# A Flamingo block on one core: row maxima turned in one instruction and sent in four transfers, softmax denominators kept in 128 columns, the first layer-norm deviations on VectorE

## The reference, cut to what matters

```python
# x, ctx: (4, 1024, 512); 16 heads of 32
q = _layernorm(x).reshape(B, T, 16, 32); k = v = ctx.reshape(B, T, 16, 32)
q = q * cos + rotate_half(q) * sin
k = k * cos + rotate_half(k) * sin
scores = jnp.einsum('bqhd,bkhd->bhqk', q, k) * scale + alibi_bias
attn = jax.nn.softmax(scores, axis=-1)
x = x + jnp.tanh(g_xattn[0]) * jnp.einsum('bhqk,bkhd->bqhd', attn, v)
# then a quantized feed-forward part: w_gate, w_up (1536 x 512) in 4 bits by blocks of 32,
# activations in 16 bits with one scale over the whole tensor, sigmoid in 16 bits, w_down
x = x + jnp.tanh(g_ffn[0]) * ffn(_layernorm(x))
```

## Time and profile before

| what | value |
| --- | --- |
| device time, median of 3 runs | 1749.58 us (1749.09 to 1751.61) |
| the profiled execution | 1751.76 us |
| its span, first to last instruction | 1749.9 us |
| busy share of the span: PE, DVE, ACT, POOL | 92%, 83%, 70%, 48% |
| attention, up to the first step of the feed-forward part | about 918 us |

### The profile page before, as it was taken

How to read it: one execution, slowest core, us unless ns; L and a number is a source line. 1 busy time by engine, 2 the same in 40 slices (tenths; PEclk the granted TensorE clock), 3 DMA queues, 4 the chain that set the end, 5 groups by cost and what they waited for, 6 DMA issues and landing times. The chain is left out here.

```text
span 1749.9 us, 37267 instructions
## 1 busy us (share of the span) xinstructions
PE 1602.6 (92%) x14821; PEld 637.6 (36%) x14821; DVE 1449.6 (83%) x2082; ACT 1221.1 (70%) x1941; POOL 838.9 (48%) x504
## 2 busy tenths in 40 slices
PE   3899999999999999999979999999999950899999
PEld 0233333333333333333325444444444420344444
DVE  7899999999999888888857998868989989755451
ACT  3688888888889888988753332329997987754450
POOL 5699899999999999998740010100000000000000
PEclk9999999999999999999999999999999975899999
DMA  6678889888799787877577898649998999986661
GB/s 156 154 149 174 169 173 182 158 170 173 152 176 182 149 175 160 171 156 140 115 175 189 266 261 271 219 153 324 347 348 275 335 354 387 287 277 216 217 217 60
DMA packets 377182, 367.94 MB, mean 210 GB/s; under 512 B 217872, under 2 KB 288912, under 8 KB 369072
## 3 DMA queue, kind: packets, MB, share of 16 engines
q1 hardware_dynamic: 368080, 300.55, 61.8%
q0 software_dynamic: 8928, 65.02, 19.0%
HBM read 154.08 MB, written 95.42 MB: 143 GB/s over the span
## 5 line engine op out<-in xcount | busy, mean ns | idle before, releaser
L1463 DVE TENSOR_REDUCE cm<-quad 128x1 f16<-128x1024 f32 x512 | 600.2, 1214 | 64.8 <-PE quad L1005 63.9
L1244 ACT ACTIVATE P<-quad 128x512 f32<-128x512 f32 x1024 | 556.8, 598 | 114.0 <-PE quad L1018 102.2
L2072 POOL TENSOR_TENSOR Ps<-P,P 128x2048 f32<-128x2048 f32 x93 | 440.6, 4738 | 45.2 <-ACT P L1244 45.2
L1018 PE MATMUL quad<-QA,KA 101*32 101x512 f16 x4096 | 366.1, 385 | 6.8 <-ACT P L1244 5.3
L1005 PE MATMUL quad<-KA,QA 100*32 100x512 f16 x4096 | 334.3, 391 | 35.6 <-DMA QA<-S 18.1
L1069 PE MATMUL quad<-P,cg 128*32 128x512 f32 x2048 | 265.5, 594 | 0.0
L1097 PE MATMUL quad<-x_hl,Wg 128*128 128x512 f16 (+1 forms) x1200 | 249.1, 370 | 1.3 <-DVE x_hl L1759 1.0
L1097 PE MATMUL quad<-x_hl,Wu 128*128 128x512 f16 x1152 | 248.8, 379 | 0.0
L1158 PE MATMUL quad<-Wd,oh 128*128 128x512 f16 x768 | 228.6, 379 | 0.0
L1018 PEld LDWEIGHTS quad<-QA,KA 101*32 101x32 f16 x4096 | 105.1, 94 | 299.3 <-ACT P L1244 231.1
L1325 ACT ACTIVATE ev<-quad 128x1024 f32<-128x1024 f32 x95 | 96.2, 1013 | 109.3 <-PE quad L1097 103.3
(11 more groups left out here) (169 smaller groups left out, 1938.3 us busy)
## 6 DMA issues: line engine op xcount, KB each, us to landing
Ps<-P POOLq DMA_DIRECT2D x62, 1024.0 KB, 8.1
gate_scratch<-ev SPq DMA_DIRECT2D x48, 512.0 KB, 3.8
gt<-gate_scratch SPq DMA_DIRECT2D x48, 512.0 KB, 5.6
up_scratch<-ev SPq DMA_DIRECT2D x48, 512.0 KB, 4.3
ud<-up_scratch SPq DMA_DIRECT2D x96, 256.0 KB, 3.6
x_words<-up_scratch SPq DMA_DIRECT2D x45, 512.0 KB, 11.4
gated_scratch<-gq SPq DMA_DIRECT2D x48, 256.0 KB, 4.1
gd<-gated_scratch SPq DMA_DIRECT2D x96, 128.0 KB, 4.3
```

What stands on the lines that cost most here:

```text
L1018: mm = e.matmul(K.score[h % 2][j:j + 32, :], K.KA[p % 2][0:101, kt, h, j:j + 32], K.QA[p % 2][0:101, 4 * qc:4 * qc + 4, h, :], start=True, ...
L1244: e.activation(K.Pb[pb][:, h, :], K.score[h % 2], ACT.Exp, scale=SCALE / (QPOW * KPOW)).then_inc(K.a_exp, 1)
L1463: e.tensor_reduce(cm[:, col:col + 1], K.quad[UNIT["max", hm, u] % 2][:, :], AX.X, ALU.max).then_inc(K.v_max, 1)
L2072: e.tensor_tensor(K.Ps[n][:, :, :], K.Pb[(st.g - 1) % NP][:, :, :], K.Pb[st.g % NP][:, :, :], ALU.add).then_inc(K.g_sum, 1)
```

## The change

It has three parts.

1. **Maxima.** `crow` is 128x32; one VectorE transpose over 128 partitions turns each 32x32 block in place of four transposes over 32 partitions, so the rows of queries 32i to 32i+31 lie in partitions 32i and on. Four DMAs carry them, each 16 pieces of 32 values (64 bytes) where one DMA had 16 pieces of 256 bytes. The semaphore `d_crow` counts 64 for a half-task.
2. **Denominators.** In place of ones a matrix `pick` stands (128x4x32, with ones in column `qt` of block `qt`). Each call of `denominators` has four matmuls of 128 queries for each head, where it had one of 512; all add into the same 128 columns, and row `qt` of a head's 32 partitions holds queries 128 `qt` and on. `den` and `denT` have 128 columns, one transpose in place of four turns `denT`, and the reciprocal reads its 16 values at other places.
3. **First deviations.** For the first four row tiles GpSimd does two steps (add, power), and VectorE does five (`first_deviations`), ahead of its step on the bias. For all later tiles nothing changes. GpSimd's other counts on `g_r1` are lower by 8, and `v_first` replaces `v_rope0`.

```diff
@@ -281,7 +281,7 @@
 
 def r1_no(b):
 
-    return 2 * R1 * (b + 1)
+    return 2 * R1 * (b + 1) - BY_VECTOR
 
 
 def w_no(m, k):
@@ -303,6 +303,7 @@
 
 
 R1, R2 = 10, 9
+FIRST, BY_VECTOR = 5, 8
 
 
 def r2_no(b):
...
@@ -350,7 +351,7 @@
 
         self.quad = quad = [ctx.enter_context(nc.psum_tensor(f"quad{i}", [128, 1024], F32)) for i in range(4)]
         self.score = [quad[2][:, 0:512], quad[2][:, 512:1024]]
-        self.num, self.den = quad[3][:, 0:512], quad[3][:, 512:1024]
+        self.num, self.den = quad[3][:, 0:512], quad[3][:, 512:640]
 
         A = Arena(nc)
         self.ident = A("ident", [128, 128], F32)
@@ -382,7 +383,7 @@
 
-        self.ones = A("ones", [128, HD], F32)
+        self.pick = A("pick", [128, 4, HD], F32)
         self.seventh = A("seventh", [128, 1], F32)
@@ -395,12 +396,12 @@
         self.biasT = A("biasT", [128, 8, 4, 16], F16)
         self.numT = A("numT", [128, 512], F32)
-        self.denT = A("denT", [128, 512], F32)
+        self.denT = A("denT", [128, 128], F32)
         self.cm = [A(f"cm{i}", [128, 32], F16) for i in range(2)]
-        self.crow = [A(f"crow{i}", [32, 128], F16) for i in range(2)]
+        self.crow = [A(f"crow{i}", [128, 32], F16) for i in range(2)]
...
@@ -717,9 +718,10 @@
 
     def write_rows(hf):
         p, qc, k = hf // 2, hf % 2, hf % 2
-        e.wait_ge(K.v_row, 4 * hf + 4)
-        row = K.QA[p % 2][100:101, 4 * qc:4 * qc + 4, :, :].rearrange("o i h q -> o (i h) q")
-        e.dma_start(row, K.crow[k][0:16, :]).then_inc(K.d_crow[k], 16)
+        e.wait_ge(K.v_row, hf + 1)
+        for i in range(4):
+            row = K.QA[p % 2][100:101, 4 * qc:4 * qc + 4, :, 32 * i:32 * i + 32].rearrange("o i h q -> o (i h) q")
+            e.dma_start(row, K.crow[k][32 * i:32 * i + 16, :]).then_inc(K.d_crow[k], 16)
 
     def load_weight(m, k):
         z, use, old = K.w_buffer(m, k)
@@ -1013,7 +1015,7 @@
         if n > 2:
             e.wait_ge(K.a_exp, n - 2)
         if kt == 0 and h == 0:
-            e.wait_ge(K.d_crow[hf % 2], 16 * (hf // 2) + 16)
+            e.wait_ge(K.d_crow[hf % 2], 64 * (hf // 2) + 64)
         for j in range(0, 128, 32):
             mm = e.matmul(K.score[h % 2][j:j + 32, :], K.KA[p % 2][0:101, kt, h, j:j + 32],
                           K.QA[p % 2][0:101, 4 * qc:4 * qc + 4, h, :], start=True, stop=True)
@@ -1036,10 +1038,15 @@
                 e.wait_ge(K.g_sum, sum_no(hf, n))
             else:
                 e.wait_ge(K.d_acc[n // 2], 16 * hf + 16)
-        for h in range(4):
-            if (hf, n, h) == (NHALF - 1, 3, 2):
+        Ps, last = K.Ps[n % 2 if hf == NHALF - 1 else n], n == (3 if hf == NHALF - 1 else 2)
+        halves = ((0, 1), (2, 3)) if (hf, n) == (NHALF - 1, 3) else ((0, 1, 2, 3),)
+        for heads in halves:
+            if heads == (2, 3):
                 e.wait_ge(K.v_sum, 5)
-            mm = e.matmul(K.den[32 * h:32 * h + 32, :], K.ones[:, :], K.Ps[n % 2 if hf == NHALF - 1 else n][:, h, :], start=n == 0, stop=n == (3 if hf == NHALF - 1 else 2))
+            for qt in range(4):
+                for h in heads:
+                    mm = e.matmul(K.den[32 * h:32 * h + 32, :], K.pick[:, qt, :], Ps[:, h, 128 * qt:128 * qt + 128],
+                                  start=n == qt == 0, stop=last and qt == 3)
         mm.then_inc(K.pe_den, 1)
 
     before = None
@@ -1071,13 +1078,14 @@
             mm.then_inc(K.pe_pv, 1)
         if st.out is not None:
             hf = st.out
-            for half, src, sem, done in ((0, K.denT, K.a_den, K.pe_tden), (1, K.numT, K.a_num, K.pe_tnum)):
-                ps = K.bank(("out", hf), half)
-                e.wait_ge(*K.bank_release(("out", hf), half))
-                e.wait_ge(sem, hf + 1)
-                for i in range(4):
-                    mm = e.transpose(ps[:, 128 * i:128 * i + 128], src[:, 128 * i:128 * i + 128], ident)
-                mm.then_inc(done, 1)
+            e.wait_ge(*K.bank_release(("out", hf), 0))
+            e.wait_ge(K.a_den, hf + 1)
+            e.transpose(K.bank(("out", hf), 0)[:, 0:128], K.denT[:, :], ident).then_inc(K.pe_tden, 1)
+            e.wait_ge(*K.bank_release(("out", hf), 1))
+            e.wait_ge(K.a_num, hf + 1)
+            for i in range(4):
+                mm = e.transpose(K.bank(("out", hf), 1)[:, 128 * i:128 * i + 128], K.numT[:, 128 * i:128 * i + 128], ident)
+            mm.then_inc(K.pe_tnum, 1)
         if st.s != 1 and st.dens is not None:
             denominators(*st.dens)
         before = st
@@ -1183,9 +1191,9 @@
             n = 8 * b + i
             if i == 0:
                 e.wait_ge(K.d_xg[p % 4], 16 * (p // 4) + 16)
-                e.wait_ge(K.g_r1, R1 if p == 0 else r1_no(b))
+                e.wait_ge(*((K.v_first, FIRST) if p == 0 else (K.g_r1, r1_no(b))))
...
@@ -1459,15 +1467,14 @@
             if hm < 2:
                 e.wait_ge(K.v_cm, hm + 1)
             else:
-                e.wait_ge(K.v_row, 4 * hm - 4)
+                e.wait_ge(K.v_row, hm - 1)
         e.tensor_reduce(cm[:, col:col + 1], K.quad[UNIT["max", hm, u] % 2][:, :], AX.X, ALU.max).then_inc(K.v_max, 1)
 
     def turn_rows(hm):
         e.wait_ge(K.v_max, max_no(hm, 15))
         if hm >= 2:
-            e.wait_ge(K.d_crow[hm % 2], 16 * (hm // 2))
-        for i in range(4):
-            e.transpose(K.crow[hm % 2][:, 32 * i:32 * i + 32], K.cm[hm % 2][32 * i:32 * i + 32, :]).then_inc(K.v_row, 1)
+            e.wait_ge(K.d_crow[hm % 2], 64 * (hm // 2))
+        e.transpose(K.crow[hm % 2][:, :], K.cm[hm % 2][:, :]).then_inc(K.v_row, 1)
 
     def low_part(p, w, half):
         rows = slice(4 * half, 4 * half + 4)
@@ -1506,25 +1513,40 @@
...
+    def first_deviations():
+        mean, rs, nm = K.mv1[:, 0:4, 0], K.rs1[:, 0:4], K.nm1[:, 0:4]
+        shifted, guess, square, factor = [t[:, 0:4] for t in K.nwt]
+        e.wait_ge(K.g_r1, 2)
+        e.tensor_tensor(square, guess, guess, ALU.mult).then_inc(K.v_first, 1)
+        e.wait_ge(K.v_first, 1)
+        e.tensor_tensor(factor, square, shifted, ALU.mult).then_inc(K.v_first, 1)
+        e.wait_ge(K.v_first, 2)
+        e.tensor_scalar(square, factor, -0.5, 1.5, ALU.mult, ALU.add).then_inc(K.v_first, 1)
+        e.wait_ge(K.v_first, 3)
+        e.scalar_tensor_tensor(rs, guess, QPOW / KPOW, square, ALU.mult, ALU.mult).then_inc(K.v_first, 1)
+        e.wait_ge(K.v_first, 4)
+        e.scalar_tensor_tensor(nm, mean, -1.0, rs, ALU.mult, ALU.mult).then_inc(K.v_first, 1)
+
+    first_deviations()
     e.wait_ge(K.pe_bias, 1)
     e.wait_ge(K.a_bias, 1)
     bias = K.score[0][:, 0:256].rearrange("t (i n h) -> t i n h", n=2, h=16)
     e.tensor_tensor(K.biasT[:, :, 2:4, :], bias, K.biasT[:, :, 0:2, :], ALU.subtract).then_inc(K.v_bias, 1)
     e.wait_ge(K.v_cs, 2)
     e.wait_ge(K.d_cg[1], 16)
-    first_rotation(K.cg[1], K.t1[1], slice(0, 8), 0)
+    first_rotation(K.cg[1], K.t1[1], slice(0, 8), FIRST)
     e.wait_ge(K.a_xn, 4)
-    first_rotation(K.xn, K.t1[0], slice(0, 4), 4)
+    first_rotation(K.xn, K.t1[0], slice(0, 4), FIRST + 4)
     low_part(0, 1, 1)
     low_part(0, 0, 0)
     for n in range(4, 8):
@@ -1626,12 +1648,12 @@
             hf = st.out
             p, qc = hf // 2, hf % 2
             y = K.x2s[:, 4 * qc:4 * qc + 4, :]
-            den = K.bank(("out", hf), 0).rearrange("p (i c) -> p i c", c=128)
+            den = K.bank(("out", hf), 0)[:, 0:128].rearrange("p (h c) -> p c h", c=32)
             num = K.bank(("out", hf), 1).rearrange("p (i h d) -> p i h d", i=4, d=HD)
             e.wait_ge(K.pe_tden, hf + 1)
             if hf > 0:
                 e.wait_ge(K.v_x2, hf)
-            e.reciprocal(K.rdn[:, :, :], den[:, :, 0::32]).then_inc(K.v_rec, 1)
+            e.reciprocal(K.rdn[:, :, :], den[:, 0:4, :]).then_inc(K.v_rec, 1)
             e.wait_ge(K.pe_tnum, hf + 1)
             e.wait_ge(K.v_rec, hf + 1)
             if p > 0 and qc == 0:
...
@@ -1940,7 +1962,9 @@
     e.memset(K.minus[:, :], -1.0).then_inc(K.g_half, 1)
     e.memset(K.seventh[:, :], 1.0 / 7.0).then_inc(K.g_half, 1)
     e.memset(K.twice[:, :], QPOW / KPOW).then_inc(K.g_half, 1)
-    e.memset(K.ones[:, :], 1.0).then_inc(K.g_ones, 1)
+    e.memset(K.pick[:, :, :], 0.0).then_inc(K.g_ones, 1)
+    e.wait_ge(K.g_ones, 1)
+    e.memset(K.pick[:, :, :].rearrange("p i c -> p (i c)")[:, 0:4 * HD:HD + 1], 1.0).then_inc(K.g_ones, 1)
 
     def step_of(out, a, b, op, sem, count):
@@ -1961,11 +1985,15 @@
         step_of(rs, nw[1], nw[3], ALU.mult, sem, base + 7)
 
 
+    def first_guesses():
+        e.wait_ge(K.g_half, 6)
+        e.wait_ge(K.v_mv1, 4)
+        step_of(K.nwt[0][:, 0:4], K.mv1[:, 0:4, 1], K.eps[:, 0:4], ALU.add, K.g_r1, 1)
+        step_of(K.nwt[1][:, 0:4], K.nwt[0][:, 0:4], K.half[:, 0:4], ALU.pow, K.g_r1, 2)
+
     def deviation_1(first, last, base):
         c = slice(first, last)
         w = [t[:, 0:last - first] for t in K.nwt]
-        if base == 0:
-            e.wait_ge(K.g_half, 6)
         if first == 20:
 
             e.wait_ge(K.g_r2, R2)
@@ -2034,14 +2062,15 @@
...
```

(33 more changed lines are left out.)

## The result

The change made the kernel slower. The kernel after takes **1837.92 us** (median of 4 runs, 1833.47 to 1846.93), the kernel before 1749.95 us beside it (4 runs, 1749.09 to 1751.61): a ratio of 1.0508, with a 95% interval of 1.0474 to 1.0542. That is 88 us more where 12 us less was forecast, and far outside the range of 1728 to 1748. The profiled execution took 1837.91 us, its span is 1836.1 us.

A forecast was written before the change was run, and what follows sets the result against it. No engine alone bounds the first stage, GpSimd the one between 600 and 800 us. 20 half-tasks at 0.55 us (-11.0), start -1.1, end -0.6, rows +0.7 make -12.0 from 1749.58: 1737.6 us, range 1728 to 1748.

The forecast's parts named there:

- Maxima, transfers: Four row DMAs in place of one bring the last landing 1.0 us later: 0.7 us added in all, bounds 0 and 32.
- The margin: Time between a row's landing and its need by the scores: 3.5 us to spare, 2.5 kept after the delay.
- The 32 us bound: Upper bound on the cost of the four row transfers: 32 x 1.0 us of delay.
- Maxima, VectorE: One transpose of about 0.2 us for four taking 0.90: 0.7 us less a half-task, 0.5 on the path.
- Denominators, TensorE: Small matmuls stay near streaming, 0.11 us a group of four; one transpose for four: 0.3 us less a half-task, 0.2 on path.
- Rival A: TensorE held up by handing over small matmuls in `denominators`, 0.22 us a group: +37 us, 1787 us; chance 0.11.
- ScalarE's copy, start and end: Copy of `den` 0.3 us shorter; first maxima 1.1 us earlier (bounds 0 and 1.8); copy and transposes at the end 0.6 less.
- GpSimd's stage: Between 600 and 800 us GpSimd's own work sets the pace: no gain, reciprocals unchanged at 26.9 us apart.
- Rival C: GpSimd's sums come late in all half-tasks, half of the 0.7 us gain stays: -7.7, 1742 us; chance 0.16.
- Rival B: Gain eaten up by weight loads at 0.14 us a group or rows landing late: 1746 to 1750 us; chance 0.11.

The follow-up runs named there:

- the kernel with the row last: Kernel before, with three idle small transfers issued ahead of the one transfer of the maxima's row: 1869.92 us, ratio 1.0673.
- the kernel with the row first: Kernel before, with three idle small transfers issued right behind the one transfer of the maxima's row: 1750.08 us, ratio 0.9997.
- the adding DMA behind the rotation: Kernel after, with GpSimd's adding DMA issued behind its rotation in the step and not ahead of it: 1768.02 us, ratio 1.0095.

## Why the prediction was wrong

- **Maxima, transfers: the step that failed.** It added 0.7 us, with bounds of 0 and 32. It measures 93.4 us: 1837.9 less the 1744.5 us of the kernel without part 1. The delay was nearly right: an issue takes 0.59 us, and the last follows the first by 1.8 to 3.0 us, 1.9 in the median, where 1.7 was reckoned. With the earlier turn that puts the last row, in most half-tasks, 0.7 us behind the adding DMA, where the one row was 0.3 us ahead of it: 1.0 us, as in the sum. The margin was right too: where nothing interferes, the last row lands 3.6 to 4.2 us behind the first issue and is needed 5.1 us behind it. The error was to add a delay to a landing time of 1.8 us as if the landing didn't depend on when the transfer is issued. It does: well ahead of the adding DMA a row takes 1.6 to 3.0 us, 0.4 us or more behind it 6.8 us in the median. The 32 us bound had the same fault, as it multiplied the delay and not what a delayed transfer can meet. 77.1 of the 93.4 us are the waits themselves. The clock takes its part: from 64 to 980 us the granted clock is 0.95 in the kernel after, and 1.00 in the kernel before (64 to 914), which is at most 916 x 0.05 = 46 us by estimate. The two together are 123 us, some 30 more than were lost, so the new waits must also have taken the place of idle time that was there before. No run separates these.
- **What I could have read.** The kernel before issued its row at 423.03, with the landing of the earlier trace rows, and the adding DMA at 423.39, 0.36 us behind it; every row of that kernel that had an adding DMA near was issued ahead of it, in 22 of 31 half-tasks by only 0.3 to 0.4 us. That was luck of the order, not a margin that anyone had set. Another DMA in the same 4 us, 256 times as large (1 MB against 4 KB), was in the trace, and I looked at SyncE's queue alone.
- **Maxima, VectorE: size right, gain hardly seen.** One transpose takes 0.21 us in place of 0.90. The periods of the seven half-tasks of the kernel after without a wait are 26.4 to 27.9 us, 0.26 us less on average than the same seven without part 1 (26.8 to 27.8), where 0.5 was forecast; but they follow disturbed half-tasks, so that this is a hint and no price. How much part 1 would give with its rows in time wasn't measured by itself.
- **Denominators, TensorE: right.** 0.87 us a call, 0.11 us a group of four. Rival A (0.22 us a group, 1787 us) fell, although the time went to its side. The Trainium skill's figure for a stream of weight loads and matmuls ("TensorE: Matmul & The Clock Gate", section "Back-to-back issue gap"), 81 ns each, would by estimate make a call 2.6 us; the trace has 27 ns each (0.87 us for 32), with four heads side by side.
- **ScalarE's copy, start and end.** 0.28 us for the copy, where 0.30 was forecast. The first maxima start 0.84 us earlier in the kernel after and 2.1 us earlier in the kernel without part 1, but the first rows of x arrived at different times (the fourth statistics start at 8.63 before, 9.26 and 7.97); counted from there both are 1.47 us shorter, where 1.1 was forecast with 1.8 as the bound. Parts 2 and 3 together were forecast at some -6 us (-1.1, -0.6 and 0.2 us for 20 half-tasks) and measure -6.0. Their shares weren't measured apart, so that the agreement of the sum may hold errors that cancel.
- **GpSimd's stage: right.** Between 600 and 800 us the period didn't change without part 1. Rival C isn't seen: GpSimd reaches 100% only there.
- **Rival B** named rows that land late in many half-tasks, but priced them to eat some 8 of the 12 us forecast and no more. The mechanism was on the list, its size was not, for want of the question what the row would land behind.

## What to carry to other kernels

A small transfer that something waits for has no landing time of its own: it depends on what has been issued to the DMA engines in the microseconds before it. Before such a transfer is moved or split, list every DMA from every queue that is issued within its landing time on either side, the large ones above all; a shift of 1 us past one of them can cost nearly its whole length, in each iteration, and slow TensorE's clock on top. If it has to be split, issue first what is needed first, and put the large transfer behind work that its engine has to do anyway, not behind a wait. Then look at what the large one meets in its new place: here a DMA transpose, at up to 40.7 us for one adding DMA.

## What was not expected of the hardware

- A row of 16 pieces of 64 bytes, issued 0.4 us or more behind an adding DMA of 1 MB, landed after 6.8 us in the median, 1.9 when well ahead of it. It waited for far more than one packet of 0.64 us.
- The order of four small transfers decided over some 120 us, with the same instructions (1750.08 and 1869.92 us).
- After 10 us in which TensorE was busy for 5.7, the granted clock was 0.58 over the next 4 us. In the kernel with the row last it is 0.96 and 0.94 in the two stages, in the kernel with the row first 1.00 in both.
- One adding DMA took 40.7 us, where the median of its kernel is 7.8, and the DMA transpose issued 0.30 us ahead of it took as long. No run tests which holds up which.

Open: the shares of parts 2 and 3; what a DMA transpose and an adding DMA do to each other; a kernel that protects the rows in the last half-tasks too; the adding DMA behind the rotation without part 1. None of these was measured. The fastest kernel measured is the change without its first part, 1744.49 us.
